# Batch 0 of the routing moved among the last probability scores of an attention and mixture-of-experts kernel

## What is computed

```
x = x + attention(layernorm(x))         # 16 heads of 16, causal, latent keys and values
xf = layernorm(x)                       # 4096 tokens
logits = xf @ Wr / temp                 # 8 experts
topw, topi = top_k(logits, 2); topw = softmax(topw)
for e in range(8):
    a, g = split(xf @ W1[e] + b1[e])
    y = a * silu(g) @ W2[e] + b2[e]
    out += y * (weight of expert e for the token)
return x + out
```

## Time and profile before

| | us |
|---|---|
| median of the runs | 1193.28 |
| the profiled execution | 1192.8 |
| its span | 1190.8 |
| TensorE busy | 1050.5 (88%) |
| VectorE busy | 769.9 (65%) |
| ScalarE busy | 493.6 (41%) |
| GpSimd busy | 406.8 (34%) |

### The profile page before, as it was taken

The page is one execution under the profiler, slowest core; times in us unless marked ns, Lnnn a source line. Parts: engine busy times, 40 slices in busy tenths (PEclk is TensorE's granted clock), DMA queues, the critical chain, the costliest instruction groups (busy, mean ns, idle before and its releaser), DMA issues. The chain is left out here.

```text
span 1190.8 us, 19496 instructions
## 1 busy us (share of the span) xinstructions
PE 1050.5 (88%) x5364; PEld 555.7 (47%) x5365; DVE 769.9 (65%) x2296; ACT 493.6 (41%) x1042; POOL 406.8 (34%) x770
## 2 busy tenths in 40 slices
PE   5998999999999999998576560499999999999995
PEld 2443333333333333332466460266666666666663
DVE  3777999998989999980364634255555555555552
ACT  2552377777777777777021030122222222222221
POOL 5556233333333333333204536122222222222222
PEclk9997699999999999999876655699999999999998
DMA  2879766555555555200496333123222222222222
GB/s 86 264 226 258 139 131 131 122 118 139 130 118 136 121 100 98 45 20 20 138 305 218 143 92 118 42 42 48 46 45 44 44 44 45 47 45 47 44 44 26
DMA packets 102395, 121.22 MB, mean 102 GB/s; under 512 B 26352, under 2 KB 81776, under 8 KB 102320
## 3 DMA queue, kind: packets, MB, share of 16 engines
q1 hardware_dynamic: 89024, 102.55, 34.2%
q0 software_dynamic: 13296, 17.77, 8.9%
HBM read 70.27 MB, written 49.63 MB: 101 GB/s over the span
## 5 line engine op out<-in xcount | busy, mean ns | idle before, releaser
L696 ACT ACTIVATE b_prob<-b_prob_ps 128x512 f32<-128x512 f32 (+3 forms) x768 | 310.5, 510 | 63.3 <-PE b_prob_ps L740 62.8
L722 PE MATMUL b_max_ps<-b_k_st,b_q_st 96*128 96x512 bf16 (+3 forms) x768 | 255.6, 346 | 5.7 <-DVE b_neg_max L652 1.6
L652 DVE CUSTOM_DVE_ANT_0 b_max_ps<-b_max_ps,b_mask_max 128x256 f32<-128x256 f32 (+3 forms) x512 | 241.4, 507 | 24.5 <-PE b_max_ps L722 24.4
L740 PE MATMUL b_prob_ps<-b_q_st,b_k_st 99*128 99x512 bf16 (+3 forms) x768 | 243.8, 333 | 6.3 <-ACT b_prob L696 3.1
L610 POOL TENSOR_SCALAR_AFFINE_SELECT b_prob<-b_prob 128x128 f32<-128x128 f32 x512 | 145.5, 292 | 295.3 <-ACT b_prob L696 290.3
L1414 POOL DMA_INDIRECT out_dram<-e_y,e_token x71 | 110.7, 1559 | 325.5 <-DVE e_y L1468 314.1
L655 DVE TENSOR_REDUCE b_neg_max<-b_max_ps 128x1 f32<-128x512 f32 x256 | 175.6, 686 | 13.8 <-PE b_max_ps L722 11.3
L761 PE MATMUL b_acc_ps<-b_prob,b_v_aug 128*32 128x512 f32 (+3 forms) x1536 | 143.5, 492 | 0.0
L1521 PE MATMUL e_g_ps<-w_sb,e_rowsT 128*128 x284 | 135.5, 600 | 0.3 <-issue 0.3
L1521 PE MATMUL e_a_ps<-w_sb,e_rowsT 128*128 x284 | 133.7, 593 | 0.0
L740 PEld LDWEIGHTS b_prob_ps<-b_q_st,b_k_st 99*128 99x128 bf16 x768 | 74.4, 98 | 114.4 <-ACT b_prob L696 88.5
(11 more groups left out here) (163 smaller groups left out, 1082.4 us busy)
## 6 DMA issues: line engine op xcount, KB each, us to landing
w_sb<-in_L_ffn_W SPq DMA_DIRECT2D x11, 1024.0 KB, 4.9
e_rows<-slot_rows SPq DMA_DIRECT2D x72, 129.0 KB, 2.1
ctx_cols<-b_ctx_out SPq DMA_DIRECT2D x16, 512.0 KB
q_parts<-a_part_q SPq DMA_DIRECT2D x8, 768.0 KB, 4.0
k_parts<-a_part_k SPq DMA_DIRECT2D x8, 768.0 KB, 4.8
b_q_st<-q_parts SPq DMA_DIRECT2D x16, 384.0 KB, 4.7
b_k_st<-k_parts SPq DMA_DIRECT2D x16, 384.0 KB, 7.9
a_x<-in_L_attn_x SPq DMA_DIRECT2D x8, 512.0 KB, 5.1
```

The costliest lines, as they stand in the source:

```text
L652: nc.vector.tensor_tensor_reduce(scores, scores, mask_max[:, HALF - width:HALF], -1.0, -MASKED, ALU.add, ALU.min, to).then_inc(max_done, 1)
L696: nc.scalar.activation(prob[n % NP][:, 0:width], prob_ps[n % NS][:, 0:width], ACT.Exp, scale=SCALE).then_inc(prob_ok, 1)
L722: nc.tensor.matmul(out[:, 0:width], q_st[g % RING][0:STACK, h, i * P:(i + 1) * P], k_st[g % RING][0:STACK, h, half * HALF:half * HALF + wi ...
L740: nc.tensor.matmul(prob_ps[n % NS][:, 0:width], k_st[g % RING][0:MAXROWS, h, j * P:(j + 1) * P], q_st[g % RING][0:MAXROWS, h, q0:q0 + widt ...
```

## The change

The attention's and the routing's instructions now stand in one block. The class `Route` holds what `route_phase` held, and its pieces are called from two places:

- Among the drain's slots, batch 0 as a whole, and of batch 1 the spreads and the projection. TensorE's part is put there by `between`, by slot numbers. VectorE's list goes on with routing right behind its last maximum. GpSimd makes the spread matrix at its units 170 and 172, the square root of batch 0 (with `pow`, as in the projection phase) ahead of unit 182, and the eight first scatters of batch 0, two ahead of each of its units 188 to 191. ScalarE's small Exp for batch 0 stands at its unit 186. SyncE loads for batches 0 and 1 in `sync_first` and `sync_second`.
- Behind the attention: batches 1 to 3. There the router of batch b stands ahead of the projection of batch b+1, half of which stands ahead of `counts(b)` and half behind it. ScalarE normalises the rows (`Identity` with a scale and a bias for each token) in place of VectorE.

`residual` now adds into the tile that x was loaded to, and there are two such tiles. The turned rows of batches 1 to 3 have two PSUM banks in place of one. The tiles' places in the on-chip memory are set by hand (`Room`), so that routing tiles may lie where the first two stacks of keys and queries were. `FC_EARLY` falls from 3 to 1: two of the four parts of W2 that were loaded during attention are now loaded during routing.

```diff
-FC_EARLY = 3
+FC_EARLY = 1
+SPREAD_0 = (8, 9, 10, 11)
+PROJECT_0 = (12, 13, 14, 15)
+TURN_0 = (24, 25, 26, 27)
+ROUTER_0 = (25, 26, 27, 28)
+COUNT_0 = 40
+SPREAD_1 = (42, 43, 44, 45)
+PROJECT_1 = (48, 50, 52, 54)
+SPREAD_AT = (TOTAL - 22, TOTAL - 20)
+ROOT_AT = TOTAL - 10
+POWER_AT = TOTAL - 6
+SCATTER_AT = TOTAL - 4
...
+        if g == NQUAD - 1:
+            route.sync_first(sp)
+        if g == NQUAD:
+            route.sync_second(sp)
...
+        if unit in SPREAD_AT:
+            route.spread_matrix(pool, SPREAD_AT.index(unit))
+        if unit == ROOT_AT:
+            route.inverse_root(pool)
+        if unit >= SCATTER_AT:
+            route.first_scatter(pool, (2 * (unit - SCATTER_AT), 2 * (unit - SCATTER_AT) + 1))
...
+        if unit == POWER_AT:
+            route.exponent(act, 0)
...
+                if TOTAL <= unit < TOTAL + LEAD:
+                    route.between(pe, n - TOTAL * QUAD)
...
+    def sync(self, sp):
...
+        sp.wait_ge(self.inv_den_ok, 1)
+        self.load_den(sp, 2)
+        load_w2(1)
+        for b in range(2, BATCH):
+            sp.wait_ge(self.proj_ok, b * PAIRS)
+            self.load_heads(sp, b)
...
+    def inverse_root(self, pool):
+        pool.wait_ge(self.mean_var_ok, 1)
...
+    def gpsimd(self, pool):
+        pool.wait_ge(self.pv_ok, TOTAL)
...
+        self.scatter(pool, 0, 1, self.first_row[0], self.second_in_slot)
+        for b in range(1, BATCH):
+            self.scatter(pool, b, 0, self.first_row[b % 2], self.first_in_slot[b % 2])
...
+            self.scatter(pool, b, 1, second_row, self.second_in_slot)
...
+        dve.wait_ge(self.const_ok, 6)
+        invert(0)
+        scale_heads(0)
+        residual(0)
+        moments(0)
+        invert(1)
+        dve.wait_ge(self.small_in, 48)
+        then(nc.vector.reciprocal(self.inv_temp[:], self.temp_in[:]))
+        first_normalise()
+        choose(0)
+        slots(0)
+        scale_heads(1)
+        for b in range(1, BATCH):
+            residual(b)
+            moments(b)
+            if b + 1 < BATCH:
+                invert(b + 1)
+            shift(b)
+            if b + 1 < BATCH:
+                scale_heads(b + 1)
+            choose(b)
+            slots(b)
+        tables()
...
+        act.wait_ge(self.pv_ok, TOTAL)
+        for b in range(1, BATCH):
+            act.wait_ge(self.inv_var_ok, b)
+            nc.scalar.activation(self.root[:], self.inv_var[:], ACT.Sqrt).then_inc(self.root_ok, 1)
+            normalise(b)
+            self.exponent(act, b)
+            copy(b)
...
+    def tensor(self, pe):
+        pe.wait_ge(self.prob_ok, TOTAL * QUAD)
+        pe.wait_ge(self.acc_out[1], NQUAD)
+        for b in range(1, BATCH):
+            if b + 1 < BATCH:
+                for k in range(SPREADS):
+                    self.spread_out(pe, b + 1, k)
+            for t in range(PAIRS + 1):
+                if t < PAIRS:
+                    self.turn(pe, b, t)
+                if t:
+                    self.router(pe, b, t - 1)
+            if b + 1 < BATCH:
+                for t in range(PAIRS // 2):
+                    self.project(pe, b + 1, t)
+            self.counts(pe, b)
+            if b + 1 < BATCH:
+                for t in range(PAIRS // 2, PAIRS):
+                    self.project(pe, b + 1, t)
```

More of the change, by code:

```diff
@@ L8 @@
+import math
 from contextlib import ExitStack
@@ new lines, in _, with acc_copy, rows_copy @@
+    @block.scalar
+    def _(act):
+        def acc_copy(g, half):
+            act.wait_ge(pv_ok, g * UNITS + HALF_DONE[half])
+            if g >= 2 and half == 0:
+                act.wait_ge(ctx_st[g % 2], 32 * (g // 2))
+            nc.scalar.activation(ctx_out[g % 2][:, half * HALF:(half + 1) * HALF], acc_ps[:],
+                                 ACT.Copy).then_inc(acc_out[half], 1)
+        def rows_copy(g):
+            act.wait_ge(rows_ps_ok, g + 1)
+            if g >= 2:
+                act.wait_ge(rows_in[(g - 2) % RING], 16 * PARTS * ((g - 2) // RING + 1))
+            nc.scalar.activation(max_rows[g % 2][:], turned_ps(g), ACT.Copy).then_inc(rows_ok, 1)
+        for unit in range(-LEAD, TOTAL):
+            if turned_at(unit + LEAD) is not None:
+                rows_copy(turned_at(unit + LEAD))
+            if unit < 0:
+                continue
+            g, u = divmod(unit, UNITS)
+            if u == LAG and g >= 1:
+                acc_copy(g - 1, 1)
+            if u == HALF_DONE[0] + LAG:
+                acc_copy(g, 0)
+            if unit == POWER_AT:
+                route.exponent(act, 0)
+            for n in range(unit * QUAD, (unit + 1) * QUAD):
+                width = prob_unit(block_at(n)[0] % UNITS)[3]
+                act.wait_ge(prob_sc_ok, n + 1)
+                if n >= NP:
+                    act.wait_ge(pv_ok, block_at(n - NP)[0] + 1)
+                nc.scalar.activation(prob[n % NP][:, 0:width], prob_ps[n % NS][:, 0:width], ACT.Exp,
+                                     scale=SCALE).then_inc(prob_ok, 1)
+        acc_copy(NQUAD - 1, 1)
@@ L1581 @@
+        room = Room(nc, upper.first["b_mask_max"], upper.first["b_v_aug0"])
+        expert_phase(nc, dram, room, (w1_sb, w2_sb, bias, loaded), route.ident, route.tile_expert, route.tile_row, out)
 _INS = ["L0_attn_x", "L0_attn_W_DKV", "L0_attn_W_UK", "L0_attn_W_UV", "L0_attn_W_UQ", "L0_attn_W_O", "L0_ffn_Wr",
```

1482 lines of the change are left out of this document (782 added, 700 removed).

## The result

The changed kernel took 1161.11 us (median of 4 runs, 1159.67 to 1164.11) against 1193.11 for the kernel before (4 runs, 1191.83 to 1194.07): a ratio of 0.9733, 95% interval 0.9716 to 0.9749, or 32.0 us less. The forecast was 1165.6. The profiled execution took 1161.29 us with a span of 1159.5; before it was 1192.8 and 1190.8, so the two spans differ by 31.3 us.

The account below looks back on a forecast made before the run. Routing was taken as a dependent chain with no engine full. Drain 30.0, batches 91.9 and late results 9.3 make 131.2 us against the old 158.4 from attention's end to last slots: 1192.8 - 27.2 = 1165.6 us, range 1145 to 1187.

Parts of the forecast that it names:

- The drain: End of the attention: woven-in routing work and added waits make it 30.0 us longer, bounds 19.4 and 37.
- The stall at slot 24: In the drain, TensorE waits for the first normalised rows behind GpSimd's root: 2.5 us.
- TensorE's work: In the drain: 28.9 us added at the upper clock, 2.9 of it in free time, leaving 26.0.
- The wait of spread 3: In the drain, batch 1's spread 3 waits for `scale_heads(1)` behind `slots(0)`: 0.5 us.
- Contention on GpSimd: Drain scatters, sharing memory access with VectorE: if all eight slowed, 3.4 us more, held by the upper end of 37.
- Batch 1: First routing batch behind the attention: 30.6 us, including 6.2 until its reciprocal is done.
- Batches 2 and 3: Last two routing batches: 31.7 us at a mixed clock and 29.6 at the lower clock.
- Late results: New routing: one delay of 9.3 us in reading finished results, cause unknown; bounds 0 and 27.9.
- Reservations: Outside the routing: up to 3 us behind the last slots from W2 and bias loads, at most 1 ahead of the drain.
- Rival 2: Routing batches: scatters beside TensorE's work multiply late results to 55.8 us, kernel slower at 1212.1 us; chance 0.07.
- Rival 1: Batches 1 and 2: no late result, unbroken TensorE work at the upper clock, 1141.9 us; chance 0.22.
- Rival 3: Routing: lower clock throughout and one delay per batch, no gain, 1195.6 us; chance 0.07 with what lies around it.

Follow-up runs that it names:

- experiment 3: Changed kernel with GpSimd's square root of batch 0 two units earlier: 1154.16 us, ratio 0.9643 to the kernel before.
- chip C: Chip of a later set of runs: the kernel before took 1162.18 us there, the changed kernel 1150.46, ratio 0.9896.
- A: Chip of the first measurement: the kernel before took 1193.11 us there, the changed kernel 1161.11, ratio 0.9733.
- experiment 6: Changed kernel with denominators and heads of batch 2 loaded in the drain: 1140.88 us, 9.6 under the changed kernel on the same chip.
- experiment 8: Changed kernel with both the root two units earlier and batch 2's denominators and heads loaded in the drain: 1136.34 us, 14.1 under the changed kernel on the same chip.
- experiment 4: Changed kernel with the second rows' scatter of batch 2 done twice, same rows to same slots: 1167.19 us.

## Why the prediction was right

The total is right to 4.5 us, but partly because errors cancelled. By its steps:

- **The drain.** 30.0 forecast, 31.9 measured, by luck. The stall at slot 24 was put at 2.5 us and was 3.00, with GpSimd's root as its cause; the root took 3.15 us and not 2.3, since the step of 1.05 us was read from a tile half as large and was 1.68. What I had not in the sum at all is the clock, which I took at 1.00 throughout: its fall behind the stall cost 6.8 us (experiment 3). What I had too much is TensorE's work: in experiment 3, with the clock up and 0.66 of stall, the drain grew by 22.8 us, so that the added work cost 22 at most and not 26.0. TensorE's busy time grew by 23.7 us (32.10 to 55.77) and not by 28.9: recorded ends overlap, which the lower bound of 19.4 had allowed for. The wait of spread 3 was 0.77 instead of 0.5, that of the last products for GpSimd 0.84 instead of 1.0. The counts and the matrix cost nothing, as said.
- **Contention on GpSimd.** The scatters in the drain took 0.96 to 0.98 us, one 1.25, beside VectorE's routing; the price of 3.4 us for a slower scatter did not come. The one of 1.25 was the first, at 583.17, and VectorE stood idle from 582.23 to 585.19. The page GPSIMD Engine Reference of the Trainium skill (section Specifications) names contention with, among others, VectorE's instructions that have two inputs in the on-chip memory. Beside the other seven VectorE ran residual adds, whose second input is in PSUM (L1218), statistics with one input (L1228, L1233), or nothing, so these scatters do not test that rule.
- **Batch 1.** 30.6 forecast, 28.67 measured. The reciprocal came 5.4 us behind the attention's end, by my 5.25. Spreads, turns and router took 12.7 us to the logit, my middle was 14.5: TensorE was nearer to the upper clock. The counts waited for the half projection, as said.
- **Batches 2 and 3.** 31.7 and 29.6 forecast; without late results, on chip C, 28.2 and 26.8. The level of the clock was 0.82 in batch 2 where I had taken 0.63, and in batch 3 the load of the table (1.28) lay hidden. With the late results they were 34.9 and 32.4. No table load stood between Sqrt and the Identity passes, which began at 607.78, 637.02 and 671.51 us. The Trainium skill's page ScalarE: Activation LUTs says in its section on table sets that identity is in every set, and the trace agrees.
- **Late results.** One of 9.3 us forecast; they took 6.7 and 5.6, 12.3 in all, in two batches, if the difference between chips A and C is put down to them. Size and number were a guess.
- **Reservations.** None came: 28.06 us behind the last slots and 434.90 for the experts, as before, and the drain began 0.95 us earlier.
- **The sum.** Drain +1.9, batches without late results 83.4 + 0.3 instead of 91.9, so -8.2, late results +3.0, start -0.95: 4.3 under the forecast for the profiled execution, which took 1161.29.

**Where the prediction was blind.** It took the old 158.4 us as fixed. But the kernel before holds late results too. On C, where the changed kernel shows none, the change is worth 11.7 us and not 32. The medians of the two chips differ by 30.9 us for the kernel before and by 10.6 for the changed one, so some 20 us of the gain go with the chip. That these 20 are late results avoided is my reading, but there is no profile of before on C to show it. Rival 2, late results multiplied in the new order, did not come: batch 1 has none, and the new kernel loses less from C to A than the old one. Rival 1's unbroken stretches at the upper clock came true only where the gap ahead of batch 1 was gone (experiment 6). Rival 3 needed every term at its end, and none was.

## What to carry to other kernels

When a dependent chain is woven into another stage's slots, look for the piece that stalls the engine that sets the pace. Here a stall of 3 us, with the fall of the clock behind it, made the drain 9.1 us longer, and moving one producer two units earlier took that away; of it 7.0 us were left in the profiled span on the same chip (experiment 8 against 6) and 4.5 in the medians. The same holds for loads: a wait of 6 us ahead of a stage cost 9, and the granted clock of the stage rose from 0.76 to 0.91 without it. And compare on one chip, and on more than one: the same pair of kernels differed by 32 us on one chip and by 12 on another.

## What the runs showed of the hardware

- In four of five sets of runs short dependent steps came late while indirect scatters were issued or shortly after, most of them 13 to 22 us behind the start of 16 in a row, from TensorE to ScalarE, from TensorE to VectorE and within VectorE. Against the same batches on chip C the changed kernel's took 6.7 and 5.6 us longer, and batch 2 of experiment 4 8.5. In the fifth set, on chip C, there were none, with the same transfers.
- TensorE was granted 0.50 from 559 to 576 us, busy for 16.81 us of them, behind 3.00 us idle, and stayed at 1.00 in experiment 3 with 0.66 us idle at the same place.
- On GpSimd the power of 128x8 f32 values took 1.68 us, of 128x4 1.05; the steps without it took 0.20 to 0.26.
- ScalarE's Identity pass with scale and bias over 128x256 f32 took 0.52 us each (2.08 for four), with no table load between Sqrt and it.
